# A graph network kernel: the summing stage's sums in the buffer of the states, and eight picked columns, two chunks ahead, in the first GAT pass

## What is computed

```python
def _L0_gnn_ref(...):
    att_scores = sigmoid(concat([head, rel]) @ att_w + att_b)
    aggr_emb = segment_sum(att_scores * tail, edge_index[0])
    return tanh(aggr_emb @ W_w.T + W_b)

def _gat_layer(x, src, dst, W, a_src, a_dst, b, n):
    h = x @ W
    logit = leaky_relu((h @ a_src)[src] + (h @ a_dst)[dst], 0.2)
    alpha = _segment_softmax(logit, dst, n)
    return segment_sum(alpha[:, None] * h[src], dst) + b
```

## Time and profile before

| | us |
|---|---|
| median of 3 runs | 14073.66 |
| lowest, highest run | 14048.91, 14075.56 |
| span of the profiled execution | 14084.2 |
| PE busy | 6814.7 (48%) |
| DVE busy | 7042.7 (50%) |
| ACT busy | 5152.3 (37%) |
| POOL busy | 7724.8 (55%) |

### The profile page before, as it was taken

One profiled execution on the slowest core, in us unless ns is written; L12 is line 12 of the kernel. 1 busy time (PEld: TensorE's weight loads), 2 busy tenths in 40 slices (PEclk: granted clock), 3 DMA queues, 4 the chain that ended last, 5 costly groups with the idle time before them and its releaser, 6 DMA issues. The chain is left out here.

```text
span 14084.2 us, 100376 instructions
## 1 busy us (share of the span) xinstructions
PE 6814.7 (48%) x27637; PEld 5669.8 (40%) x27637; DVE 7042.7 (50%) x12322; ACT 5152.3 (37%) x5609; POOL 7724.8 (55%) x7576
## 2 busy tenths in 40 slices
PE   5443366657756774777577646661111322232222
PEld 5433355545545553655455535551111211121111
DVE  5333345434444443444444546663444466646666
ACT  0011144444434443444344424442222243423432
POOL 7888755544444445344444455546665555545553
PEclk7555577768777776887677767775555565556555
DMA  5333322212211221122133323333332344434442
GB/s 154 36 36 33 58 51 58 56 39 55 54 49 42 56 55 42 48 55 55 40 90 91 86 72 97 97 89 89 115 109 96 116 143 136 140 94 141 138 140 81
DMA packets 782270, 1137.56 MB, mean 81 GB/s; under 512 B 500471, under 2 KB 559955, under 8 KB 774499
## 3 DMA queue, kind: packets, MB, share of 16 engines
q0 software_dynamic: 355008, 370.44, 14.1%
q1 hardware_dynamic: 363245, 417.03, 9.6%
q10 hardware_dynamic: 63926, 349.09, 6.2%
HBM read 680.14 MB, written 468.70 MB: 82 GB/s over the span
## 5 line engine op out<-in xcount | busy, mean ns | idle before, releaser
L970 POOL DMA_INDIRECT turned<-d_t,idx x5788 | 5465.9, 944 | 5006.3 <-DVE wide L1426 3228.1
L1115 PE MATMUL banks<-pair,hot 128*128 128x462 f32 x16184 | 3981.1, 402 | 1677.0 <-issue 1661.2
L1115 PEld LDWEIGHTS banks<-pair,hot 128*128 128x128 f32 x16184 | 3357.4, 208 | 2299.7 <-issue 1921.1
L1236 DVE TENSOR_TENSOR wide<-banks,member 128x462 f32<-128x462 f32 x1156 | 689.9, 634 | 2788.3 <-remote 2123.6
L1084 ACT COPY wide<-wide 128x952 f32<-128x952 f32 (+2 forms) x252 | 503.4, 1997 | 2831.5 <-DVE wide L1446 2800.7
L650 POOL DMA_INDIRECT d_acc<-work,idx x784 | 1237.7, 1579 | 263.9 <-issue 234.4
L733 ACT ACTIVATE hot<-keys,row 128x1024 fp32r<-128x1024 f32 (+1 forms) x1036 | 1073.1, 1117 | 277.9 <-PE banks L1115 204.9
L1171 PE MATMUL banks<-ident,wide 128*128 128x128 f32 x588 | 163.1, 423 | 1814.2 <-issue 945.2
L1446 DVE TENSOR_TENSOR_SCAN wide<-banks,wide 128x224 f32<-128x224 f32 (+4 forms) x1288 | 1036.9, 871 | 5.8
L1128 PE MATMUL banks<-pair,hot 128*128 128x448 f32 x3136 | 804.7, 417 | 452.1 <-issue 393.8
L1128 PEld LDWEIGHTS banks<-pair,hot 128*128 128x128 f32 x3136 | 688.1, 221 | 568.7 <-issue 492.5
(11 more groups left out here) (311 smaller groups left out, 9556.1 us busy)
## 6 DMA issues: line engine op xcount, KB each, us to landing
d_e<-wide ACTq DMA_DIRECT2D x168, 924.0 KB
turned<-d_t,idx POOLq DMA_INDIRECT x5788
d_e<-wide ACTq DMA_DIRECT2D x84, 1008.0 KB
wide<-d_b SPq DMA_DIRECT2D x60, 1344.0 KB
keys<-d_key SPq DMA_DIRECT2D x124, 512.0 KB
d_b<-wide SPq DMA_DIRECT2D x28, 1344.0 KB
wide<-d_edge SPq DMA_DIRECT2D x84, 448.0 KB
d_em<-wide ACTq DMA_DIRECT2D x84, 448.0 KB
```

The source lines that it names most:

```text
L970: gp.indirect_dma_start(rows[:, b, k, :], None, table[:, :], offset(idx[:, b, k:k + 1])).then_inc(s["gathered"][b], 16)
L1115: mm = nc.tensor.matmul(ps_cols[i], hot[:, place, i, j, :], flat(g.pair[:, part, j]), start=(j, part) == (0, 0), stop=(j, part) == (SETS - ...
L1236: nc.vector.tensor_tensor(found[:, i - i0], ps_cols[i].rearrange("p (w c) -> p w c", c=SET), mid(member[:, i], TW), ALU.mult).then_inc(pic ...
```

## The change

The summing stage's `agg` is no longer a tile of its own but `g.h`, which the first pass of states does not need yet. Its writers (L1665 on DVE, L1796 on ACT) thus write rows of 64 elements with a pitch of 128, and its readers read them. The first GAT pass has X = 8 and `ahead=2`. All lines between the removed one (L662) and L1492 have a number one lower in the new file.

```diff
 COLS = {"gat": 8, "dot": 4}
-FIRST_COLS = 7
...
-    def __init__(self, nc, g, ph, kind, ahead, cols=None):
-        X = self.X = cols or COLS[kind]
+    def __init__(self, nc, g, ph, kind, ahead):
+        X = self.X = COLS[kind]
...
     if lent:
         tiles.update(tmp=[P, GC, KF], out=[P, C, out_w - KF], kf=[P, KF_RING, GC, KF])
-        del tiles["agg"]
     elif out is None and out_w:
         tiles["out"] = [P, C, out_w]
+    if lent or summing:
+        del tiles["agg"]
...
-    agg = g.h if lent else tiles["agg"]
+    agg = g.h if lent or summing else tiles["agg"]
...
-                nc.vector.tensor_tensor(agg[:, cols, :].rearrange("p c f -> p (c f)"), sums[:, 0, 0],
-                                        sums[:, 1, 0], ALU.add).then_inc(s["summed"], 1)
+                totals = sums[:, :, 0].rearrange("p t (c f) -> p t c f", f=D)
+                nc.vector.tensor_tensor(agg[:, cols, :], totals[:, 0], totals[:, 1], ALU.add).then_inc(s["summed"], 1)
...
-                nc.scalar.activation(agg[:, slice(*groups[j]), :].rearrange("p c f -> p (c f)"),
-                                     ps_mix[:, 0:GC * D], ACT.Tanh).then_inc(s["activated"], 1)
+                nc.scalar.activation(agg[:, slice(*groups[j]), :], ps_mix[:, 0:GC * D].rearrange("p (c f) -> p c f", f=D),
+                                     ACT.Tanh).then_inc(s["activated"], 1)
...
-            layer(nc, g, dict(kind="sum", rows=g.x, w_o=a["l0_w"], **std), dict(kind="gat", ahead=0, cols=FIRST_COLS))
+            layer(nc, g, dict(kind="sum", rows=g.x, w_o=a["l0_w"], **std), dict(kind="gat", ahead=2))
```

More of the change, by code:

```diff
@@ L775, in widen_maxima, with edges @@
     return nc.vector.tensor_copy(out[:, width:width + heads], maxima)
-def edges(nc, g, ph, banks, rows, tiles, ready, kind, pk=None, a=None, update=False, clear=None, ahead=0, cols=None):
+def edges(nc, g, ph, banks, rows, tiles, ready, kind, pk=None, a=None, update=False, clear=None, ahead=0):
     H = NH if kind == "multi" else 1
@@ L1897, in layer @@
         ph.now = ph.block()
-        pk = Picks(nc, g, ph, edge["kind"], edge["ahead"], edge.get("cols")) if edge and edge["kind"] in COLS else None
+        pk = Picks(nc, g, ph, edge["kind"], edge["ahead"]) if edge and edge["kind"] in COLS else None
         ready = nodes(nc, g, ph, banks, turned, wide, pk=pk, **node)
```

## The result

The changed kernel takes 14152.64 us (median of 4 runs, 14145.39 to 14158.32) against 14074.61 us for the kernel before in the same comparison (4 runs, 14048.91 to 14085.67). The ratio is 1.006, with a 95% interval of 1.0046 to 1.0074: 78.0 us slower. The profiled execution has a span of 14156.3 us against 14084.2, 72.1 more.

What follows compares the result with a forecast made beforehand. Each chunk was taken as bound by a chain of gathers, picked columns and product, no engine near full. Start +27.9, chunks +57.1 and buffer 0 made +85.0 us on 14073.66: 14158.7, range 14115 to 14195.

Steps and rivals of the forecast that it cites:

- Part 1, the buffer of the states: Summing stage: writing 64 elements at a pitch of 128 costs 0, with less than 1 us either way.
- Part 2, the chunks: Pass 1, first to last product: 27 intervals rise from 973.8 to 1031.0 us, +57.1, between +54.5 and +59.8.
- my band of 1028 to 1034: Pass 1 after the change: expected time in us from its first product to its last.
- The cause named for it: Chunks: the fourth column ahead of the product is late, as PE hardly works during the gathers' second half; 4.7 us in one chunk.
- three columns are finished before it begins: Chunks: three picked columns are done before PE's slow stretch during the gathers, and a fourth is not.
- the chain that it describes: Chunks in both forms: gathers end, DVE gets its picked columns, the product runs and frees rows for the next gathers.
- Part 3, the start: Start of pass 1: 28 columns needed instead of 10 move the first product from 1855.95 to 1883.8 us, +27.9.
- The lower bound of 6.7: Start of pass 1: if PE is never held, the first product comes at 1862.7 us, +6.7.
- Nothing outside pass 1: Rest of the kernel: after pass 1 everything as before, 85 us later, and no change expected elsewhere.
- A start without the held stretch: Start of pass 1: without PE's slow stretch it costs 6.7 instead of 27.9, sum 64 instead of 85; counted with the forecast.
- The first rival: The gathers alone set the pass: 588 become 544, saving 55 us, 14019, faster; chance 0.04.
- The rival's condition: First rival, chunks: it decides where the fourth column is finished before PE slows.

Runs made afterwards that it cites:

- e1: Changed kernel with only the buffer edit kept, pass 1 back at seven columns, none picked ahead, three before the product: 10539.76 us against 10540.24 before, ratio 0.9999.
- f1: The changed kernel repeated without an edit in the second session: 14157.52 us, ratio 1.0062 to the kernel before.
- f2: Changed kernel with nothing picked ahead in all five passes, eight columns, four before the product: 13998.25 us, ratio 0.9948 to the kernel before.
- f3: Changed kernel, all passes (8, 0, 3): eight columns a chunk, no chunks picked ahead, three columns taken before the product; 13835.68 us, ratio 0.9835 to the kernel before.
- e2: Changed kernel with nothing picked ahead in pass 1, eight columns, four before the product: 10504.56 us, ratio 0.9967 to the kernel before.
- e4: Changed kernel, pass 1 with eight columns, none picked ahead, three before the product: 10507.44 us, ratio 0.9969 to the kernel before.
- e3: Changed kernel, pass 1 with seven columns, two chunks picked ahead, three before the product: 10564.88 us, ratio 1.0024 to the kernel before.
- g4: Changed kernel, all passes with seven columns, none picked ahead, three before the product, third session: 13664.07 us, ratio 0.9841 to the kernel before.

## Why the prediction was right

The forecast was 14158.7 us, slower; measured were 14152.64 us. Point by point, by its own steps:

- **Part 1, the buffer of the states: 0.** Right. The seven adds are spread over 58.1 us in both traces, and e1 has 0.9999.
- **Part 2, the chunks: +57.1, between 54.5 and 59.8.** 53.6 in the profiled execution (973.8 to 1027.5), 0.9 under the lower end; the 1027.5 lies 0.5 under my band of 1028 to 1034, and f1's profile has 1033.4. What carried the forecast is that pass 1 would look like the others, and it was so to 1 us in the same trace (1027.5 and 1026.8).
- **The cause named for it**, a fourth column late because PE is held: shown for the greater part. f2 keeps the cost with nothing picked ahead (1029.8), f3 gives back 37.5 of the 56 us by moving one column, and e2 with e4 show no such cost where PE isn't held. The other 18.5 us are still there in f3. The prediction's "three columns are finished before it begins" holds in pass 1 of before only: in the chunk of the earlier trace rows and in that of the changed kernel two are, and the third lacks 3 and 5 matmuls. And the chain that it describes, gathers then product, hangs together only by the held stretch, not by data.
- **Part 3, the start: +27.9, between 6.7 and 39.** 29.5 by the trace, the first product at 1888.84 for 1884. f2 has the same term from the other side, 27.6. The 24th gather was followed by the first product after 81.9 us, forecast as 80. The lower bound of 6.7 set a start without the held stretch against one with it, a pair that no run has. Where neither has it, e3 against e1, picking two chunks ahead made the first product 36.3 us later.
- **Nothing outside pass 1.** So in kind. In number, +3.4 us came from ahead of the summing stage and -18 from passes 2 to 5, neither from code that differs. They, and 4.0 behind pass 5, are the reason why the sum of +85.0, with 86.5 measured at the last product of pass 1, met a span that grew by only 72.1 and a median that grew by 78.0.
- **A start without the held stretch**, by which the sum would have been 64: the measured 78.0 lies nearer to 85, and the start's own term was 29.5 and not 6.7. PE was held in the start as behind the earlier trace rows, from 1793 to 1811.67 us. The prediction tied this case to the Trainium skill ("Runtime: NRT & Kernel Launch", "Instruction fetch mechanics"), which says that instruction fetching is mostly hidden. Whether fetching is what PE waits for, no run shows.
- **The first rival**, the gathers alone set the pass: I gave it 0.04, and at this level it is out. It is the true account of the chunks in the first session, though not of the start: picking two chunks ahead moved the first product by 36.3 us there (e3). I had read "PE is held during gathers" as a property of the kernel, and it depends on the session as well. The forecast is right for this level alone; I had no ground for the level. The rival's condition, a fourth column that is finished before PE slows, is the one that e2 met.

Open: the changed kernel wasn't run at the level of 10540 us. Worked out there, e2's -35.7 and e3's +25.1 over e1 make -11, no change to be seen. Open too: what holds PE and DVE while gathers run, and why one chip has it in one session and not in another. In the chunks read, the held stretch of PE begins 15 to 19 us after the first gather, and in most it ends 4.7 us after the last one starts.

**A better version** came out: f3, (8, 0, 3) in all passes, is 1.65% faster than the kernel before in the second session and 1.56% in the third. At the level of 10540 us only its pass 1 was run (e4, 0.31% faster). g4 is as fast in the third session, but where the gathers bind, seven columns in a single pass cost 35 us against eight (e1 and e2), so f3 is the safer one to take. g4 wasn't run in the second session, where a pass of its form took 974 us against 992.

## What to carry to other kernels

- If the form that an edit brings already runs elsewhere in the same trace, read its cost there, first to last event of the loop; both large terms here came from such rows within 4 us. It holds for the level that the trace was taken at.
- Ask of each piece in a batch whether the step that frees the next transfers waits for it. One column more ahead of the product cost 2 us a chunk, though all engines were half idle; moved behind the product it cost 0.7 (992.3 us a pass against 973.8), and moving a second one, in a batch of its own, made it worse again.
- Work done ahead of a loop fills its start. Picking two chunks ahead cost 25 to 32 us a pass more than it gave back.
- If a stall ends on nothing the trace names, compare the versions in several sessions: their order can depend on a condition that no source line shows.

## What the hardware did that I hadn't expected

- The same kernel took 10540.24 us and 14069.81 us on the same chip in two sessions, a ratio of 1.335, while the runs of each session lie within 0.4% of each other. Runs that agree within one session don't tell at which level it is.
- At the slower levels PE issued matmuls 1.4 to 3.5 us apart, mostly 2.8, with no wait in the records while indirect gathers were issued, and the granted clock fell to 0.50 in it; DVE had idle times of mostly 10 to 17 us ended by nothing named. At the faster level neither is there: of PE's 118.9 us idle ahead of these matmuls in pass 1 of e1, 118.7 are waits for DVE or ACT. A gather is issued each 1.249 us at both.
- Of DMA work the two levels have the same (1991 and 1986 us of packet time on the gathers' queue), so it is the engines' work that stands still, not the transfers that take longer. The two queues of kind "instruction" on the page also moved the same, 0.51 and 0.48 MB in e1 and 0.52 and 0.48 in the kernel before.
